# Graph network of four layers: x loaded over another queue, node numbers made on GpSimd, and a scalar carried past the merge of layer 1

## The reference

```python
h = jnp.maximum(_layernorm(x, axis=-1), 0.0)
x = x + _L0_gnn_ref(h, L0_gnn_weight, L0_gnn_bias, edge_index, edge_weight)   # hyperbolic, weighted edges
h = jnp.maximum(_layernorm(x, axis=-1), 0.0)
x = x + _L1_gnn_ref(h, edge_index, L1_gnn_W, L1_gnn_b, L1_gnn_mag_w, L1_gnn_mag_b, L1_gnn_attn_w)   # softmax attention
h = jnp.maximum(_layernorm(x, axis=-1), 0.0)
x = x + _L2_gnn_ref(h, edge_index, L2_gnn_W, L2_gnn_a)                        # exponential attention
h = jnp.maximum(_layernorm(x, axis=-1), 0.0)
x = x + _L3_gnn_ref(h, src, dst, L3_gnn_w_neigh, L3_gnn_w_self, L3_gnn_b_self) # mean of neighbours
```

```python
agg = jax.ops.segment_sum(h_src * attn_weights[:, None], tgt, num_segments=N)
h_combined = h + agg
h_poincare = _expmap0(h_combined)            # tanh(norm) * u / norm
norms = jnp.linalg.norm(h_poincare, axis=1, keepdims=True)
return jnp.where(norms > MAX_NORM, h_poincare * (MAX_NORM / (norms + 1e-08)), h_poincare)
```

## Time and profile before

| | us |
|---|---|
| median of three runs (4918.93 to 4925.36) | 4919.24 |
| the profiled execution's own time | 4916.51 |
| its span in the trace | 4914.3 |
| busy: GpSimd | 3237.7 (66%) |
| busy: VectorE | 3201.9 (65%) |
| busy: TensorE | 3102.4 (63%) |
| busy: ScalarE | 1812.3 (37%) |

### The profile page before, as it was taken

The page is one execution under the profiler, slowest core; times in us unless marked ns, Lnnn a source line. Parts: engine busy times, 40 slices in busy tenths (PEclk is TensorE's granted clock), DMA queues, the critical chain, the costliest instruction groups (busy, mean ns, idle before and its releaser), DMA issues. The chain is left out here.

```text
span 4914.3 us, 56189 instructions
## 1 busy us (share of the span) xinstructions
PE 3102.4 (63%) x11120; PEld 2159.2 (44%) x11120; DVE 3201.9 (65%) x10216; ACT 1812.3 (37%) x4295; POOL 3237.7 (66%) x3382
## 2 busy tenths in 40 slices
PE   1788888885454666665545556656666666666665
PEld 1566666563332333333333444444443544444443
DVE  7999999999864666666676555555557544444445
ACT  4555555556872333333346433333336200000000
POOL 1777777773007777777762777777772577777776
PEclk6989999987776777777777787788887878778787
DMA  4544444443044333433334545445454544434434
GB/s 153 137 131 131 132 132 133 131 131 105 1 116 108 106 106 105 107 105 106 106 98 136 132 132 132 131 130 133 133 132 136 148 113 113 114 105 113 113 106 144
DMA packets 290664, 586.89 MB, mean 119 GB/s; under 512 B 63201, under 2 KB 170717, under 8 KB 290334
## 3 DMA queue, kind: packets, MB, share of 16 engines
q0 software_dynamic: 159456, 440.74, 33.8%
q1 hardware_dynamic: 99472, 108.21, 7.0%
q10 hardware_dynamic: 31406, 34.36, 2.5%
HBM read 530.98 MB, written 52.10 MB: 119 GB/s over the span
## 5 line engine op out<-in xcount | busy, mean ns | idle before, releaser
L494 POOL DMA_INDIRECT X<-table,src_tab x2490 | 2383.7, 957 | 1275.2 <-issue 715.2
L619 PE MATMUL psum<-X,onehot 128*128 128x259 f32 x4980 | 1726.1, 493 | 883.0 <-ACT onehot L760 365.5
L619 PEld LDWEIGHTS psum<-X,onehot 128*128 128x128 f32 x4980 | 1105.8, 241 | 1304.7 <-ACT onehot L760 537.2
L1305 DVE SCALAR_TENSOR_TENSOR A<-A,psum 128x259 f32 x1660 | 702.3, 423 | 665.5 <-PE psum L619 549.7
L484 POOL DMA_INDIRECT X<-table,src_tab x832 | 804.8, 967 | 348.7 <-issue 237.6
L760 ACT ACTIVATE onehot<-G,zero_col,ecols 128x128 f32<-128x128 bf16 x1660 | 686.8, 481 | 652.3 <-PE psum L619 504.4
L1305 DVE SCALAR_TENSOR_TENSOR A<-A,same_tab,psum 128x259 f32 x1620 | 775.3, 479 | 114.3 <-PE psum L619 12.3
L628 PE MATMUL psum<-H,G 128*128 x1664 | 571.0, 430 | 193.8 <-DVE G L1395 184.1
L606 PE MATMUL psum<-X,onehot 128*128 128x259 f32 x1664 | 539.6, 409 | 4.3 <-DVE A L1305 3.6
L628 PEld LDWEIGHTS psum<-H,G 128*128 128x128 f32 x1664 | 313.8, 208 | 349.9 <-issue 309.3
L760 ACT ACTIVATE ecols<-ecols,zero_col 128x20 f32<-128x20 f32 (+2 forms) x178 | 49.9, 302 | 931.0 <-DVE ecols L1871 455.4
(11 more groups left out here) (375 smaller groups left out, 3083.2 us busy)
## 6 DMA issues: line engine op xcount, KB each, us to landing
X<-table,src_tab POOLq DMA_INDIRECT x3322, 2.8
plain<-rows_dram ACTq DMA_DIRECT2D x168, 160.0 KB, 3.3
plain<-rows_dram SPq DMA_DIRECT2D x104, 256.0 KB, 3.4
table<-H SPq DMA_DIRECT2D x21, 906.5 KB, 5.8
x_dram<-X SPq DMA_DIRECT2D x21, 896.0 KB, 4.1
X<-x_dram SPq DMA_DIRECT2D x14, 896.0 KB, 5.2
table<-A SPq DMA_DIRECT2D x7, 906.5 KB, 6.9
G<-x_dram SPq DMA_DIRECT2D x7, 896.0 KB, 5.6
```

Source lines behind the costliest of these rows:

```text
L494: pool.indirect_dma_start(ring[:, s % SLOTS, :], None, table, bass.IndirectOffsetOnAxis(src_tab[:, s:s + 1], 0)).then_inc(sem(f"batch_in{s ...
L619: pe.matmul(psum[:, k % ACC_BANKS, 0:W], hots[:, k % HOTS, :], ring[:, k, :], start=True, stop=True).then_inc(sem("used"), 1)
L1305: stt(total, total, same, psum[:, t % ACC_BANKS, 0:W], ALU.mult, ALU.add).then_inc(sem("sum_added"), 1)
```

## The change

Three parts. First, ScalarE issues only part 0 of x and src's rows; parts 1 to 6 are issued by SyncE, two of them ahead of the weight matrices and the rest behind them. Second, the node numbers are converted on GpSimd. Third, the merge no longer scales H by `be`. With t2 the old denominator and own the exponent of the node's own edge, the new `kk` is over / (own + t2), so that A becomes A times `kk` plus H unscaled; the common scalar `be` = (own + t2) / t2 is kept, goes squared into the sums of squares and once more into `t1`. The squares of blocks 0 to 35 (SQ_ACT) stay on ScalarE, those of the other 13 go to VectorE.

```diff
-MERGES = ((0, NB),)
+SQ_ACT = 36
...
+        def x_part(eng, c):
+            a, z = c * UN, min(c * UN + UN, NB - 1)
+            eng.dma_start(X[:, a:z, :], x[a * P:z * P, :].rearrange("(b p) d -> p b d", p=P)).then_inc(sem(f"x_part{c}"), 16)
...
             sp.dma_start(wide["bb"], bias0.rearrange("(p d) -> p d", p=1).to_broadcast([P, D])).then_inc(sem("bias_in"), 16)
+            x_part(sp, 1)
+            x_part(sp, 2)
             for n, w in enumerate((w0, w1, w_neigh, w_self)):
                 sp.dma_start(wraw[:, n], w.rearrange("(c p) d -> p c d", p=P)).then_inc(sem("raw_in"), 16)
+            for c in range(3, OUTER):
+                x_part(sp, c)
+            sp.wait_ge(sem("x_padded"), 1)
+            sp.dma_start(X[0:TAIL, NB - 1, :], x[(NB - 1) * P:N, :]).then_inc(sem(f"x_part{OUTER - 1}"), 16)
...
+            pool.wait_ge(sem("iotas"), 2)
+            pool.tensor_copy(iota_part[:, :], part_i)
+            pool.tensor_copy(iota_b[:, :], iota_i)
+            pool.tensor_copy(iota_node[:, :], iota_i).then_inc(sem("numbers_made"), 1)
...
-            def scale_own(lo, hi):
-
-                pool.wait_ge(sem("shares"), len(MERGES))
-                for b in range(lo, hi):
-                    pool.tensor_scalar(H[:, b, 0:D], H[:, b, 0:D], col("be")[:, b:b + 1], None, ALU.mult).then_inc(sem("own_scaled_late"), 1)
...
-                if q == 0:
-                    scale_own(*MERGES[-1])
...
-            x_part(0)
+            act.sem_inc(sem("act_go"), 1)
+            x_part(act, 0)
             rows_in(act, src, src_rows_i, "src_padded", 1, "src_in")
-            x_part(1)
             act.sem_inc(sem("turned_kept"), 4)
             act.sem_inc(sem("coef_ready"), 2)
-            act.wait_ge(sem("dst_in"), 16 * (3 + EC))
-            for c in range(2, OUTER):
-                x_part(c)
-            act.wait_ge(sem("x_padded"), 1)
-            act.dma_start(X[0:TAIL, NB - 1, :], x[(NB - 1) * P:N, :]).then_inc(sem(f"x_part{OUTER - 1}"), 16)
             act.wait_ge(sem("small_consts"), 1)
...
+            merge_exps()
+            for b in range(SQ_ACT):
+                square_sum(b)
...
-            dve.wait_ge(sem("iotas"), 3)
-            dve.tensor_copy(iota_node[:, :], iota_i)
-            dve.tensor_copy(iota_b[:, :], iota_i)
-            chain(dve.tensor_copy(iota_part[:, :], part_i))
...
             dve.tensor_copy(col("x2"), H[:, :, AUX2])
+            dve.wait_ge(sem("numbers_made"), 1)
             dve.sem_inc(sem("rows0_free"), 1)
...
                 chain(ts(t2, t2, 1e-10, None, ALU.add))
-                chain(dve.reciprocal(t2, t2))
-                chain(tt(over, over, t2, ALU.mult))
+                chain(tt(own, own, t2, ALU.add))
+                chain(dve.reciprocal(own, own))
+                chain(tt(over, over, own, ALU.mult))
+                dve.reciprocal(t2, t2)
+                chain(dve.reciprocal(own, own))
                 chain(tt(own, own, t2, ALU.mult))
-                ts(own, own, 1.0, None, ALU.add).then_inc(sem("shares"), 1)
...
+            def square_combined(b):
+                dve.wait_ge(sem("combined"), b + 1)
+                stt(junk[:, b % UN, :], A[:, b, 0:D], 1.0, A[:, b, 0:D], ALU.mult, ALU.mult,
+                    accum_out=col("aa")[:, b:b + 1]).then_inc(sem("squared_dve"), 1)
...
+            for b in range(NB):
                 combine(b)
+                if b > SQ_ACT:
+                    square_combined(b - 1)
+            square_combined(NB - 1)
...
-            dve.wait_ge(sem("squared"), 5 * NB)
+            tt(col("t4"), col("be"), col("be"), ALU.mult).then_inc(sem("share_square"), 1)
+            dve.wait_ge(sem("share_square"), 1)
+            dve.wait_ge(sem("squared_dve"), NB - SQ_ACT)
+            dve.wait_ge(sem("squared"), 4 * NB + SQ_ACT)
+            chain(tt(col("aa"), col("aa"), col("t4"), ALU.mult))
...
             chain(tt(col("t1"), col("t1"), col("t4"), ALU.mult))
+            chain(tt(col("t1"), col("t1"), col("be"), ALU.mult))
```

More of the change, by code:

```diff
@@ L865, in elu_parts, with merge_exps @@
                     func(H[:, b - 1, 0:D], H[:, b - 1, 0:D], ACT.Exp, scale=-1.0).then_inc(sem("elu_exp"), 1)
-            def merge_parts(m):
-                lo, hi = MERGES[m]
-                act.wait_ge(sem("gaps"), m + 1)
-                func(col("kk")[:, lo:hi], col("kk")[:, lo:hi], ACT.Exp)
-                func(col("be")[:, lo:hi], col("be")[:, lo:hi], ACT.Exp).then_inc(sem("gap_exps"), 1)
-            def scale_own(m, b):
-                act.wait_ge(sem("shares"), m + 1)
-                func(H[:, b, 0:D], H[:, b, 0:D], ACT.Identity, scale=col("be")[:, b:b + 1]).then_inc(sem("own_scaled"), 1)
-            def merges(s):
-                for m, (lo, hi) in enumerate(MERGES[:-1]):
-                    at = s - (LT + hi)
-                    if at == 4:
-                        merge_parts(m)
-                    if 0 <= at - 8 < hi - lo:
-                        scale_own(m, lo + at - 8)
-                    if 0 <= at - 14 < hi - lo:
-                        square_sum(lo + at - 14)
+            def merge_exps():
+                act.wait_ge(sem("gaps"), 1)
+                func(col("kk"), col("kk"), ACT.Exp)
+                func(col("be"), col("be"), ACT.Exp).then_inc(sem("gap_exps"), 1)
             def weighted(q):
@@ L1074, in _ @@
             weighted(0)
-            for m, (lo, hi) in enumerate(MERGES[:-1]):
-                for b in range(max(lo, lo + S_REAL - LT - hi - 8), hi):
-                    scale_own(m, b)
-            merge_parts(len(MERGES) - 1)
-            for m, (lo, hi) in enumerate(MERGES):
-                for b in range(lo if m == len(MERGES) - 1 else max(lo, lo + S_REAL - LT - hi - 14), hi):
-                    square_sum(b)
+            merge_exps()
+            for b in range(SQ_ACT):
+                square_sum(b)
             asked(20)
@@ L1752, in fade_first, with merge_gaps @@
                 chain(stt(blk(A, at, AUX3, W), blk(A, at, AUX, AUX + 1), drop, blk(A, at, AUX3, W), ALU.mult, ALU.add))
-            def merge_gaps(m):
-                lo, hi = MERGES[m]
-                z, peaks = A[:, lo:hi, AUX], A[:, lo:hi, AUX3]
-                t2, t3, over, own = (col(name)[:, lo:hi] for name in ("t2", "t3", "kk", "be"))
+            def merge_gaps():
+                z, peaks = A[:, :, AUX], A[:, :, AUX3]
+                t2, t3, over, own = (col(name) for name in ("t2", "t3", "kk", "be"))
                 ts(t3, z, 0.5, -BIG, ALU.is_lt, ALU.mult)
@@ L1763, in merge_gaps @@
                 chain(tt(t2, t2, t3, ALU.add))
-                chain(tt(t3, H[:, lo:hi, AUX2], H[:, lo:hi, AUX3], ALU.max))
+                chain(tt(t3, H[:, :, AUX2], H[:, :, AUX3], ALU.max))
                 chain(tt(t3, t3, t2, ALU.max))
                 tt(over, t2, t3, ALU.subtract)
-                tt(own, H[:, lo:hi, AUX2], t3, ALU.subtract).then_inc(sem("gaps"), 1)
-            def merge_shares(m):
-                lo, hi = MERGES[m]
-                dve.wait_ge(sem("gap_exps"), m + 1)
-                t2, over, own = (col(name)[:, lo:hi] for name in ("t2", "kk", "be"))
-                chain(tt(t2, A[:, lo:hi, AUX], over, ALU.mult))
+                tt(own, H[:, :, AUX2], t3, ALU.subtract).then_inc(sem("gaps"), 1)
@@ L1775, in merge_shares @@
+            def merge_shares():
+                dve.wait_ge(sem("gap_exps"), 1)
+                t2, over, own = (col(name) for name in ("t2", "kk", "be"))
+                chain(tt(t2, A[:, :, AUX], over, ALU.mult))
                 chain(tt(t2, t2, own, ALU.add))
                 chain(ts(t2, t2, 1e-10, None, ALU.add))
-                chain(dve.reciprocal(t2, t2))
-                chain(tt(over, over, t2, ALU.mult))
+                chain(tt(own, own, t2, ALU.add))
[3 more added lines that the diff above has]
+                chain(dve.reciprocal(own, own))
@@ L2009, in _ @@
             softmax_sums()
-            merge_gaps(len(MERGES) - 1)
-            for m, (lo, hi) in enumerate(MERGES[:-1]):
-                for b in range(max(lo, lo + S_REAL - LT - hi - 10), hi):
-                    combine(b)
-            merge_shares(len(MERGES) - 1)
-            for b in range(*MERGES[-1]):
+            merge_gaps()
+            merge_shares()
+            for b in range(NB):
                 combine(b)
+                if b > SQ_ACT:
+                    square_combined(b - 1)
+            square_combined(NB - 1)
             dve.wait_ge(sem("vectors_in"), 16 * 5)
```

20 lines of the change are left out of this document (removed).

## The result

The changed kernel takes 4842.89 us (median of four runs, 4840.76 to 4845.04), the kernel before beside it 4919.09 us (four runs, 4918.35 to 4925.36). The ratio is 0.9842, with a 95% interval of 0.9825 to 0.9859: faster by 1.6%, 76 us where 39 were forecast.

What follows compares the result with a forecast made beforehand. GpSimd's 3322 gathers were taken to set the pace (4141 of 4914.3 us), so only set-up and merge could move: 4916.51 - 20.5 - 18.7 = 4877.3 us, forecast as 4880 us from the runs' median, range 4870 to 4898.

Steps and rivals of the forecast that it cites:

- Set-up, 20.5 us forecast: Set-up: x's parts issued from SyncE let `fields` start at 11.1 us instead of 31.63, gaining 20.5 us (17.9 to 21.5).
- the case for which the text had 11.3 us: Set-up: `fields` starts at 11.3 us, not 10.06, if ScalarE's table load of 1.28 us does not run ahead.
- the 43 us that were allowed for: Set-up: SyncE free at 43 us if ScalarE's issuing came on top of its own; first table stores would wait 13 us.
- The data rival: Set-up: `fields` waits for data, not for ScalarE, so it starts as late as before; 4900.5 us, chance 0.06.
- Casts, 0 us: Set-up: converting node numbers on GpSimd instead of VectorE gains 0, as x's landing covers at most 1.6 us.
- Merge, 18.7 us: Merge after layer 1: shares to first update of X take 34.7 us instead of 53.37, gaining 18.7 us.
- the slow-combine rival: Merge: a combine stays at 0.70 us because of its own operands; the merge gains 4, 4894.7 us, chance 0.03.
- The gathers, 0 us: Gathers of all layers: the diff touches none, so only stretches in which GpSimd does not gather can move.
- The rival of the gathers' pace: Gathers: shifted VectorE operations hold up descriptor writing; 11.8 ns each cancels the gain, 15 ns gives 4930 us; chance 0.03.
- The two priced terms: Set-up gain of 20.5 us and merge gain of 18.7 us, together 39.2 us.

## Why the prediction was right in its terms and wrong in its sum

- **Set-up, 20.5 us forecast:** 19.3 measured, within the bounds of 17.9 to 21.5. The table load did not run ahead, the case for which the text had 11.3 us; `fields` began at 11.64 and not at 11.1. SyncE had its first table store out 10 us before the 43 us that were allowed for, and no part of x was waited for. The data rival (4900.5 us) is out: the wait for dst's rows was 0.17 us. The 25.5 us of ScalarE's stream were not all issuing, as the text had it: the issue of x at 4.14 us was over in 0.41, the next came at 13.67, and the 9 us between were the wait for dst's rows. The seven issues of x took ScalarE some 16 us, and SyncE 12 in the changed kernel; the gain comes from taking both, the wait and the issues, away from ahead of the root. The Trainium skill's DMA: Bandwidth & Descriptors ("Issuing engines are not separate DMA queues") calls what another issuer saves, the sequencer's time to initiate a DMA, usually small beside the transfer. In this trace it was not small: single issues of ScalarE lasted up to 4.9 us (the one at 18.06), and a part's transfer is 2.7 us by the prediction's estimate.
- **Casts, 0 us:** the change with and without them lies within the scatter (4839.29 against 4842.89 us). They took 0.19 to 0.29 us each.
- **Merge, 18.7 us:** 53.37 - 34.26 = 19.1 measured, the new path 34.26 where 34.7 was worked out. Combines of 0.48 us refute the slow-combine rival (4894.7 us). ScalarE's last square was over some 5 us before VectorE's, as said.
- **The gathers, 0 us:** this step failed. The text said that the diff touches no gather, so that only stretches without gathers can move. The rows say -35.7 us, 10.8 ns a gather from start to start. The step took the duration of an unedited instruction for fixed by that instruction. The runs show that it also hangs on which other operations stand between the layers' gathers in GpSimd's program: 946 ns with none or with products of two tensors, 957 with 49 multiplications by a column of scalars. Which mechanism of GpSimd makes it so stays open.
- **The rival of the gathers' pace** named the right quantity, 11.8 ns a gather for the whole gain, and the wrong sign. It looked for a cause in phases and VectorE's traffic and held it at 0.03 because nothing in the loops is edited. A range that took this bound both ways, 39.2 us below the forecast as well as above it, would have reached 4840.8 and held the result.

The two priced terms give 38.4 us of the 39.2 forecast; with 35.7 for the gathers and some 3 us lost at the joints of the stages (from the table), the span's 71.1 us are accounted for.

## What to carry to other kernels

Where thousands of equal instructions of one engine pace a kernel, read their duration again after every edit to that engine's program, wherever it stands: 1% of 957 ns was worth as much as a whole stage. Between GpSimd's gathers, try the same arithmetic as a product of two tensors, or on another engine, before counting a multiplication by a column of scalars as hidden. And price issuing DMAs, and the waits that stand among the issues, as the issuing engine's own time: some 16 us of issues and 9 of a wait on ScalarE held up one root that took 0.30.

## What was not expected of the hardware

- A gather's own time has levels that no view of one kernel shows: 946, 949, 953 and 957 ns for the same instruction, steady over a whole layer, and different from kernel to kernel. The Trainium skill's GPSIMD Engine Reference ("2.1 Instruction dispatch") describes a resident dispatcher that finds the entry of each instruction's opcode and calls it, at tens of cycles per instruction, and a further cost at the first call of a freshly loaded kernel. As described there, neither cost hangs on which other operations the program has. Here the gathers' time does, by way of the execution ahead or of something fixed at loading.
- On GpSimd, a product of two tensors of 128x256 (one of them a column spread along the row) starts every 0.745 us, a multiplication by a column of scalars every 0.900, both beside VectorE's combines.
- A multiplication of 128x1 on GpSimd took 273 ns in the mean behind layer 1. Beside VectorE's set-up the mean was 559 ns, of single ones from 277 to 1686 with a median of 278: some were held up and the others were not.
